# Four conditioned residual layers on one core: layers 0 and 1 run one pair further ahead, partial products in one block of a step, PSUM banks dealt out anew

## The reference

```python
x = x + (x @ W.T + s[a] * (x @ A[a].T) @ Bm[a].T)           # layer 0: a = itok_B_0_6, one of 8 adapters of rank 16
x = x + einsum('bct,bcd->bdt', x, w1[itok_B_1_198])         # layer 1: a 64 x 64 matrix for each sequence
q, k, v = x @ Wq.T, x @ Wk.T, x @ Wv.T                      # layer 2: causal attention, 16 heads of 32
x = x + softmax(mask(min(cond, 4) * q @ k.T / sqrt(32))) @ v @ Wo.T
x = x + einsum('bct,bcd->bdt', x, w3[itok_B_0_7])           # layer 3: again 64 x 64 for each sequence
```

## Time and profile before

| | |
|---|---|
| median of 3 runs | 612.41 us (610.5 to 612.68) |
| profiled execution | 612.43 us, its span 610.6 us |
| granted TensorE clock, mean | 0.997 |
| TensorE busy | 602.3 us (99%) |
| VectorE busy | 392.6 us (64%) |
| ScalarE busy | 224.6 us (37%) |
| GpSimd busy | 109.8 us (18%) |

### The profile page before, as it was taken

One profiled execution on the slowest core, in us unless ns is written; L12 is line 12 of the kernel. 1 busy time (PEld: TensorE's weight loads), 2 busy tenths in 40 slices (PEclk: granted clock), 3 DMA queues, 4 the chain that ended last, 5 costly groups with the idle time before them and its releaser, 6 DMA issues.

```text
span 610.6 us, 21490 instructions
## 1 busy us (share of the span) xinstructions
PE 602.3 (99%) x8524; PEld 519.9 (85%) x8524; DVE 392.6 (64%) x573; ACT 224.6 (37%) x434; POOL 109.8 (18%) x101
## 2 busy tenths in 40 slices
PE   8999999899999999999999999999999999999998
PEld 8898889788898988889888898988889898888885
DVE  4799865665657566575765657567575766646374
ACT  4446342342424334251443424344251443513222
POOL 2013120301203030040402204040030302103030
PEclk9999999899999999999999999999999999999999
DMA  8962313222322322222231322322222231310212
GB/s 288 174 131 69 99 41 82 67 63 73 75 65 76 91 73 60 73 62 75 73 67 71 90 75 53 86 73 61 73 63 73 75 87 49 69 68 3 71 41 104
DMA packets 65273, 48.29 MB, mean 79 GB/s; under 512 B 16923, under 2 KB 51739, under 8 KB 65243
## 3 DMA queue, kind: packets, MB, share of 16 engines
q1 hardware_dynamic: 60090, 42.63, 26.8%
q10 hardware_dynamic: 5152, 5.24, 2.9%
HBM read 30.54 MB, written 17.30 MB: 78 GB/s over the span
## 4 chain that ended last, share of the span: by engine, by line
PE 97%; DVE 1%; DMA 1%; issue 1%; ACTq 0%; ACT 0%; DVEq 0%
PE banks L649 10%; PE banks L654 10%; PE banks L650 10%; PE banks L677 5%; PE banks L748 5%; PE banks L755 5%; PE banks L679 5%; PE banks L681 5%; PE banks L749 5%; PE banks L589 5%; PE banks L591 5%; PE banks L593 5%; PE banks L702 5%; PE banks L694 4%; PE banks L718 3%; PE banks L616 3%
## 5 line engine op out<-in xcount | busy, mean ns | idle before, releaser
L649 PE MATMUL banks<-x1T_hi,w_hi 128*128 128x256 f32 x512 | 129.8, 286 | 0.0
L650 PE MATMUL banks<-x1T_hi,w_lo 128*128 128x256 f32 x512 | 128.2, 283 | 0.0
L649 PEld LDWEIGHTS banks<-x1T_hi,w_hi 128*128 128x128 f32 x512 | 98.0, 191 | 0.7 <-ACT x1T_hi L914 0.4
L650 PEld LDWEIGHTS banks<-x1T_hi,w_lo 128*128 128x128 f32 x512 | 98.1, 192 | 0.0
L654 PE MATMUL banks<-x1T_lo,w_hi 128*128 128x256 f32 x512 | 82.4, 283 | 0.0
L1428 POOL TENSOR_TENSOR probs<-probs,row_max 128x1024 f32<-128x1024 f32 x32 | 61.0, 1906 | 112.5 <-DVE row_max L1209 112.5
L1410 POOL TENSOR_TENSOR w_own<-w_in,own 128x128 f32<-128x128 f32 x32 | 14.7, 460 | 364.6 <-PE banks L616 267.6
L654 PEld LDWEIGHTS banks<-x1T_lo,w_hi 128*128 128x128 f32 x512 | 70.6, 192 | 0.2 <-DVE x1T_lo L1120 0.2
L1195 DVE TENSOR_TENSOR qkT<-banks,beta 128x512 f32<-128x512 f32 x32 | 22.1, 690 | 59.4 <-PE banks L654 59.4
L914 ACT ACTIVATE x_y<-banks 128x512 f32<-128x512 f32 (+1 forms) x17 | 9.9, 585 | 128.8 <-PE banks L616 122.0
L1213 DVE TENSOR_REDUCE row_sum<-probs 128x16 f32<-128x1024 f32 x32 | 39.0, 1218 | 25.0 <-ACT probs L996 25.0
(11 more groups left out here) (138 smaller groups left out, 1054.1 us busy)
## 6 DMA issues: line engine op xcount, KB each, us to landing
x_rows<-x_in SPq DMA_DIRECT2D x64, 128.0 KB, 2.4
x_kept<-x_rows SPq DMA_DIRECT2D x16, 512.0 KB, 3.6
x_in<-in_x_dram SPq DMA_DIRECT2D x60, 128.0 KB, 2.8
out_dram<-x_y SPq DMA_DIRECT2D x15, 512.0 KB, 3.0
b_sel<-b_parts SPq DMA_DIRECT2D x180, 32.0 KB, 1.7
w_in<-in_L_cond_weights_dram SPq DMA_DIRECT2D x128, 16.0 KB
probsT<-in_L_cond_W_dram ACTq DMA_DIRECT2D x1, 1024.0 KB, 6.1
probs<-in_L_cond_Wk_dram ACTq DMA_DIRECT2D x1, 1024.0 KB, 7.8
```

Of the source, the lines that this page charges most:

```text
L649: nc.tensor.matmul(out_ap, w_hi[:, w, c, cols], x1T_hi[:, c, :], start=(c == 0), stop=False)
L650: nc.tensor.matmul(out_ap, w_lo[:, w, c, cols], x1T_hi[:, c, :], start=False, stop=False)
```

## The change

TensorE's step is reordered. Layer 0 and layer 1 now run for pair `i+2` in step `i`, and `adapters_down` for pair `i+3`. The order in a loop step is: values, `layer0(i+2)`, `turn_probs(i, 0)`, `layer2_out(i-1)`, `turn_probs(i, 1)`, keys, queries, then in one block `adapters_down(i+3)`, `layer3(i-1)`, `attend`, `scores(i+1)`, `layer1` of pair `i+2`. Layer 0 writes to `SC[0:2]` (`L0`), queries to `OUT`, attention to `MIX`, `adapters_down` to `SC[2]` (`OUT[1]` for pair 2), and the transposed probabilities swap banks between the head groups. Layers 0 and 1 of pair 1 and `adapters_down(2)` move to the setup, where layer 0 writes to `MIX`. Before the last product of `scores`, TensorE waits for `attn_split` and for what layer 1 reads. ScalarE, VectorE and SP are reordered to match: SP gathers `w1` before `b_sel`, both for pair `i+3`, and gathers `b_sel` of pair 2 before step 0. GpSimd's program is the same. The core of the diff, in this order: banks, SP's step, `scores`, TensorE's step, TensorE's setup.

```diff
-X1T, Q, AT = SC[0:2], (OUT[0], MIX[0]), (OUT[1], MIX[1])
+X1T, L0, Q, AT = SC[0:2], SC[0:2], OUT, MIX
+DOWN_2, DOWN = OUT[1], SC[2]
-DOWN = OUT[1]
...
+        def turned_banks(g):
+            return SC[2:4] if g == 0 else SC[0:2]
...
+            gather_own_b(2)
             def step(i):
                 if after(i, 3):
                     turned_in(i + 3)
-                if after(i, 2):
-                    gather_own_b(i + 2)
+                    gather_w1(i + 3)
+                    gather_own_b(i + 3)
                 if after(i, 1):
                     store_x1(i + 1)
-                if after(i, 3):
-                    gather_w1(i + 3)
...
                                 for j in range(JG):
                                     m, rows = 2 * mm + h, slice(j * HD, (j + 1) * HD)
+                                    if after(i, 1) and after(i, -1) and (mm, t, r, h, j) == (1, TILES - 1, SEQT - 1, 1, JG - 1):
+                                        pe.wait_ge(attn_split, SEQT * i)
+                                        layer1_ready(i + 1)
...
-                layer0(i + 1)
-                if not prev:
-                    values(i, 1, x0_of=i + 1)
-                    layer1()
-                pe.wait_ge(probs_done[0], i + 1)
-                turn_probs(i, 0, range(7))
-                turn_probs(i, 0, range(7, 8))
-                if prev:
-                    if nxt2:
-                        pe.wait_ge(v_copied, TILES * (i + 1))
-                        adapters_down(i + 2, x0_of=i + 1)
-                    layer1()
+                if nxt2:
+                    pe.wait_ge(s_masked, HG * i + 1)
+                    layer0(i + 2)
+                else:
                     for t in range(TILES):
                         layer2_out(i - 1, t)
+                pe.wait_ge(s_masked, HG * (i + 1))
+                pe.wait_ge(probs_done[0], i + 1)
+                turn_probs(i, 0, range(8))
+                if prev and nxt2:
+                    for t in range(TILES):
+                        layer2_out(i - 1, t)
+                pe.wait_ge(probs_done[1], i + 1)
                 if nxt2:
-                    pe.wait_ge(probs_done[1], i + 1)
-                    turn_probs(i, 1, range(8))
+                    pe.wait_ge(x0_copied_act, i + 3)
+                    pe.wait_ge(x0_copied_dve, i + 3)
+                turn_probs(i, 1, range(8))
...
                 for m in range(NC):
-                    if m == 2:
-                        pe.wait_ge(x1_copied, SEQT * (i + 1))
                     key_part(i + 1, m)
...
                     query_part(m)
                     if m == (1 if parted(i) else 3):
+                        pe.wait_ge(k_copied_act, i + 2)
+                        pe.wait_ge(k_copied_dve, i + 2)
+                        if nxt3:
+                            adapters_down(i + 3)
                         if prev:
                             layer3(i - 1)
...
+                if nxt3:
+                    pe.wait_ge(xa_summed, i + 3)
                 scores(i + 1)
+                if nxt2:
+                    layer1()
...
                 query_part(m)
-            adapters_down(1)
+                if m == 1:
+                    adapters_down(1)
+            pe.wait_ge(k_copied_act, 1)
+            pe.wait_ge(k_copied_dve, 1)
+            layer0(1)
             scores(0)
+            adapters_down(2)
+            layer1_ready(1)
+            layer1()
```

More of the change, by code:

```diff
@@ L333, in y_banks, with down_bank, layer0_banks @@
             return SC[0:2] if after(i, 2) else OUT
+        def down_bank(i):
+            return bank[DOWN_2 if isinstance(i, int) and i == 2 else DOWN]
+        def layer0_banks(i):
+            return MIX if isinstance(i, int) and i < 2 else L0
+        def turned_banks(g):
+            return SC[2:4] if g == 0 else SC[0:2]
         def last_attn(ap, t, r):
@@ L607, in adapters_up @@
                     pe.wait_ge(xa_lo_placed, i)
-                nc.tensor.matmul(bank[MIX[t]][:], xa_parts[:, t, :], b_sel[:, t, :],
-                                 start=False, stop=True).then_inc(x0_mm, 1)
+                nc.tensor.matmul(bank[layer0_banks(i)[t]], xa_parts[:, t, :], b_sel[:, t, :], start=False, stop=True)\
+                    .then_inc(x0_mm, 1)
             def mix(rows_of, w_own, out_banks, done):
@@ L666, in query_part, with values @@
                     last.then_inc(q_mm, 1)
[L668 to L673, removed]
+            def values(i, t):
+                if not after(i, -1) and t == 1:
+                    pe.wait_ge(xa_summed, 2)
                 for c in range(NC):
-                    if x0_of is not None and c == NC - 1:
-                        layer1_ready(x0_of)
                     nc.tensor.matmul(bank[OUT[t]][:], x1T_hi[:, c, tok(t)], w_hi[:, WV, c, :],
@@ L945, in xa_low_part @@
                 act.wait_ge(xa_mm, i + 1)
-                copy(xa_low[:], bank[DOWN][half(1), 0:P]).then_inc(xa_low_done, 1)
+                copy(xa_low[:], down_bank(i)[half(1), 0:P]).then_inc(xa_low_done, 1)
             def xa_hi_part(i):
@@ L961, in x0_copy @@
                 act.wait_ge(x0_mm, TILES * i + 1)
-                copy(x0[:, 0, :], bank[MIX[0]]).then_inc(x0_copied_act, 1)
+                copy(x0[:, 0, :], bank[layer0_banks(i)[0]]).then_inc(x0_copied_act, 1)
             def first_x1_copy():
@@ L1094, in _ @@
             load_blocks(act, WO, Wo)
-            for n in (0, 1):
-                part_hi(n)
-            copy_k(0)
-            for n in (2, 3):
-                part_hi(n)
-            x_hi(1)
             act.wait_ge(turned_lo, GROUP_A + 1)
@@ L1103, in _ @@
             select_a(1)
+            for n in PARTS_V:
+                part_hi(n)
+            copy_k(0)
+            x_hi(1)
             xa_low_part(1)
             xa_hi_part(1)
+            select_a(2)
+            x0_copy(1)
+            xa_low_part(2)
+            x_hi(2)
             in_steps(act, step)
@@ L1139, in sum_xa @@
                 dve.wait_ge(xa_low_done, i)
[L1140 removed]
+                nc.vector.tensor_tensor(xa_sum[:], down_bank(i)[half(0), 0:P], xa_low[:], ALU.add)\
                     .then_inc(xa_summed, 1)
@@ L1161, in x0_copy @@
                 dve.wait_ge(x0_mm, TILES * (i + 1))
-                copy(x0[:, 1, :], bank[MIX[1]]).then_inc(x0_copied_dve, 1)
+                copy(x0[:, 1, :], bank[layer0_banks(i)[1]]).then_inc(x0_copied_dve, 1)
             def first_x1_copy():
@@ L1270, in step @@
                         part_lo(n)
-                    copy_k(1)
-                if nxt2:
-                    xa_lo_part(i + 2)
-                    x_lo(i + 2)
-                if after(i, 3):
-                    turn_x(i + 3)
-                if prev:
-                    copy_k(i + 1)
+                copy_k(i + 1)
                 scale_q(i + 1, range(1))
@@ L1389, in _ @@
                 turn_w(n)
+            copy_k(0)
             turn_x(1)
-            for n in PARTS_V:
-                part_lo(n)
-            copy_k(0)
-            scale_q(0)
+            scale_q(0, range(1))
             x_lo(1)
@@ L1398, in _ @@
             xa_lo_part(1)
+            scale_q(0, range(1, 2))
+            for n in PARTS_V:
+                part_lo(n)
+            turn_x(2)
+            x0_copy(1)
+            sum_xa(2)
+            scale_xa(2)
+            x_lo(2)
             in_steps(dve, step)
```

156 lines of the change are left out of this document (55 added, 101 removed).

## The result

The changed kernel takes 627.65 us (median of 4 runs, 626.88 to 631.47) against 611.88 us for the kernel before in the same comparison: a ratio of 1.0273, 95% interval [1.0226, 1.0319]. It is slower by 2.7%. The forecast was 623.4 us in a range of 613 to 636. The profiled execution took 627.63 us with a span of 625.9, so 15.3 us more span than before.

A forecast was written before the change was run, and what follows sets the result against it. TensorE, busy 99% of the span, bounds the kernel. Loop +3.7, steps 0, 13, 14 -0.6, setup +0.2, b_sel +2.7, keys +2.0, q_scaled -0.4, clock +3.4 give +11.0 on 612.4: 623.4 us, range 613 to 636.

The forecast's parts named there:

- Fewer changes of the array: Every step: one block of partial products instead of two saves one switch pair, 0.20 us a step, bounds 0 and 0.20.
- The jump: End of the loop body: with layer 1 last, the loop's jump hides, saving 0.19 us a step, bounds 0 and 0.19.
- The wait for attn_split: Loop steps: the last score product waits for attn_split, costing 0.70 us in each of 12 steps, bounds 0.57 and 0.8.
- b_sel in step 0: Layer 0 of pair 2 in step 0: TensorE waits 2.7 us for b_sel, issued behind gather_w1(2) on SP's queue.
- copy_k in step 0: Step 0, in front of adapters_down(3): TensorE waits 2.0 us because VectorE is late with the copy of the keys.
- The removed wait for q_scaled: Step 0: the wait of 0.44 us for q_scaled goes, a gain of 0.4 us.
- The clock: Step 0: two longer gaps each bring a fall to half clock, 3.4 us in all, bounds 0 and 3.4.
- Rival (c): End of the loop body: savings on jump and array changes exceed the wait, giving 606 to 608 us; chance 0.10.

The follow-up runs named there:

- the first experiment: The kernel before with one line more: in the loop steps the last product of scores waits for attn_split of the same step; 619.58 us against 612.49.
- the second: The changed kernel with attention of the loop steps in the OUT banks instead of MIX and layer3 ahead of adapters_down; 622.31 us against 612.49.
- the filler: The changed kernel with six idle products, results overwritten, in front of layer 1 in the setup and in step 13; 627.99 us against 611.87.
- the one with everything mended: Changed kernel with loop attention in OUT, layer 1 behind values in steps 0 and 14, copy_k(1) and b_sel gather earlier, VectorE reordered; 618.43 us against 611.87.
- the last variant: Changed kernel with layer 1 behind the values in every step, copy_k(1) ahead of part_lo, b_sel gather for pair 2 ahead of w1; 615.65 us against 611.87.

## Why the prediction came out right, and where its terms were off

The direction and the chief mechanism were right: a wait that TensorE meets in every loop step, shown alone by the first experiment and taken away by the second. The sum was 11.0 us; the measured difference is 15.8 between the medians and 15.3 between the spans. But a good part of the agreement is luck, as the terms show:

- *Fewer changes of the array.* Forecast -0.20 us a step, measured -0.22 (0.18 at the transposes, 0.04 at the output products). The prediction had set against it that every change of tiling mode costs alike, which would give 0.10. adapters_down (0.58), mix (1.02) and, where nothing jumps, layer 1 (1.09) kept their length inside the block. Attention there takes 0.08 more (below); if that belongs to the changes, the gain is 0.14 and lies between the two.
- *The jump.* Forecast -0.19, measured -0.07: layer 1 takes 1.21 us in the loop and 1.09 where nothing jumps, so 0.12 of the jump still shows.
- *The wait for attn_split.* Forecast 0.70, measured 2.26 (532.23 - 529.97, in step 12) - 1.52 = 0.74. The 0.57 of the lower bound was rightly not taken.
- *Not foreseen in the loop:* attention takes 1.49 us instead of 1.41. It is so in all variants that wait for xa_summed behind it in the loop, and not in step 0, where adapters_down stands in front of it all the same (76.71 - 75.30 = 1.41). That this wait is the reason was not tried. Together 0.74 - 0.07 - 0.22 + 0.08 = 0.53 a step where +0.31 was forecast: over twelve steps 6.4 instead of 3.7. (In the first of them a gap called issue stands in place of the wait.)
- *b_sel in step 0.* Forecast 2.7, measured nothing in the changed kernel. A hole of this kind is there when TensorE comes on time, and was covered here: SP issued from 49.07 to 56.50, 1.3 to 2 us sooner than forecast, and the gap in the setup's layer 1 and its neighbours made TensorE 1.9 us later. Where layer 1 was moved away the hole was there (1.97 us), and SP's order removed it.
- *copy_k in step 0.* Forecast 2.0, measured 1.79. The removed wait for q_scaled went as forecast, with a gap of 0.25 called issue in its place.
- *x0_copy in step 0.* Not in the sum: 0.84 (the 16 transposes hold TensorE for 64.14 - 61.40 = 2.74 us, before for 1.90). The prediction counts VectorE's work from x0_copy on and has no wait for x0_copy itself.
- *The clock.* Forecast 3.4 for two falls in step 0, measured none there in the profiled execution. This step failed. In the first loop step it fell as before, but for longer: it was 0.50 in the three windows from 122 to 128 us, where before two windows showed 0.50 and 0.65.
- *The gaps inside layer 1* are the term that was missing: 1.46 in the setup, 1.86 in step 0, 1.4 in step 13, and of the 1.5 lost in loop steps 1 and 2 the larger part. I had the clue in the earlier trace rows, a gap called issue amid scores the first time the loop body ran, and took it for something that stays as it is. They come only the first time that code is run: from the second loop step on there is none in the same block. Splitting the block took them away in the setup, step 0 and step 13. It is not the length of the joined block that decides: it has 344 passes in a row in the loop, but 208 in the setup and 192 in steps 0 and 13, and there the gap comes after 186, 178 and 140 of them; and the filler moved the gaps by its own 12 passes. Their places lie at fixed counts of passes since the start, with 77 + 50 = 127 passes between the two gaps of step 0 and 106 + 21 = 127 between those of the first loop step. What the change did was to put small products on more of these places. The trace also shows what happens there: ahead of each such gap one packet of 16 KB on a queue of kind "instruction" (the last section has the lines). That is theory B, TensorE's instructions arriving too late, with the supply in pieces. The filler of step 13 stood behind such a place, where the gap had already come, and so helped by 0.5 us only. No run changed the supply itself.
- *A rival's figure.* Rival (c) says 606 to 608, but its own terms, 612.4 - 8.0, give 604.4 for the lower end. Nothing hangs on it: the time went the other way.

So of 15.3 us, the loop's steady price is 6.4, step 0's late results 2.6, and some 6 are gaps of the last kind and the clock behind them. That the total came within 4.3 us is luck in part: it owes much to terms that were wrong in opposite directions: 6.1 us (b_sel and clock) were forecast and did not come, and about 6 were not forecast and did.

## What to carry to other kernels

Before groups on TensorE are joined, ask which engine must empty the banks that the next group writes, and how long after the last product that is done: a result that comes 2.1 us after attention cost nothing behind 4.5 us of work (scores and half of the values), and costs 0.74 us behind the 1.5 us of scores alone. Attention's result in banks that nobody needs for 2.6 us was worth 0.65 us a step. Where code runs for the first time, products of 11 to 17 ns a pass can outrun the supply of TensorE's own instructions, while whole products of 0.23 us did not in these traces. So in code written out once, a long run of small products is better cut by whole-array work, and a gap called issue is looked for by its place in the count of passes. And when one gap is mended, look at what it covered: here b_sel lay behind the gap in layer 1, and x0_copy behind b_sel.

## What the hardware showed that I had not expected

- Gaps of 0.2 to 2.0 us called issue inside groups of 17 and 11 ns passes, only at the first run of code, and in all variants of the changed kernel at the same counts of passes since the start. The kernel's own transfers are not needed for them: in the setup the DMA engines were nearly idle during the gap. Windows of TensorE there (us, TensorE busy, granted clock, DMA share, GB/s):

```profile
46.00:48.00 2.00, 2.00 (x128) 1.00 0.16 32
48.00:50.00 2.00, 0.91 (x36) 1.00 0.00 1
```

- What goes ahead of such a gap is a fetch of code. DMA queues of the changed kernel in the windows 82.0:84.0 (step 0) and 121.5:123.5 (first loop step), just ahead of the gaps that end at 84.64 and 124.28:

```profile
q8 instruction: 1, 0.02, 3.2%
...
q8 instruction: 1, 0.02, 2.9%
```

  Each is one packet of 16384 bytes that takes about 1 us. In the traces of all nine kernels the gaps called issue among scores and layer 1 end 2.2 to 2.9 us after such a packet starts (82.31 and 84.64, 121.98 and 124.28). In the window 130:540, loop steps 2 to 12, the queue has none, and no such gap comes. The 127 passes between two gaps with their 127 weight loads make 254 instructions, so 16384 / 254 = 64.5 bytes for each: an estimate that fits one packet for each such piece of TensorE's program. In step 0 such packets also fall into whole products (the one at 66.85, for example), and there no gap follows.

- The clock did not fall after gaps of 1.72 and 1.51 us in step 0 of the changed kernel, but fell to half in the same step after one of 2.01 us in the variant with attention in OUT, after 1.76 in the one with everything mended, and after 1.71 in the one with the filler. In the first loop step it fell after 1.63 us before, and stayed at 1.00 after 1.46 us in the run with the wait alone. In the last variant it fell after 1.50 us. The length of the gap alone did not decide: 1.72 was without a fall, 1.71 and 1.50 with one.

- Executions of one kernel differ in it. The kernel before had spans of 609.0 us at a mean granted clock of 1.000 and of 610.7 at 0.997; the one with everything mended 613.3 at 1.000 and 618.1 at 0.992; the changed kernel 625.9 at 0.995 and 629.7 at 0.989. One trace shows one such course, so 1.7 to 4.8 us between two traces can be the clock's alone.
